# Four of eight low one-hot groups: subtraction on GpSimd and two activations on ScalarE in place of VectorE's comparison

## The reference, cut to what matters

```python
shared = _ffn(xf, shared_gate, shared_up, shared_down)
probs = softmax(xf @ gate_w.T)
topw, topi = top_k(probs, 2)
topw = topw / (topw.sum(-1, keepdims=True) + 1e-20)
comb = zeros((T, E)).at[arange(T)[:, None], topi].add(topw)
for e in range(E):
    routed += _ffn(xf, expert_gate[e], expert_up[e], expert_down[e]) * comb[:, e][:, None]
return shared + routed
# _ffn(x, g, u, d) = silu(x @ g.T) * (x @ u.T) @ d.T
```

## Time and profile before

| | us |
|---|---|
| median of three runs | 841.98 (841.88 to 842.23) |
| profiled execution | 840.84 |
| its span, first to last instruction | 839.1 |
| busy in the span: PE | 783.3 (93%) |
| DVE | 588.7 (70%) |
| ACT | 487.4 (58%) |
| POOL | 277.0 (33%) |
| mean granted clock of TensorE | 0.987 of full |

### The profile page before, as it was taken

How to read it: one execution, slowest core, us unless ns; L and a number is a source line. 1 busy time by engine, 2 the same in 40 slices (tenths; PEclk the granted TensorE clock), 3 DMA queues, 4 the chain that set the end, 5 groups by cost and what they waited for, 6 DMA issues and landing times.

```text
span 839.1 us, 21195 instructions
## 1 busy us (share of the span) xinstructions
PE 783.3 (93%) x6686; PEld 642.8 (77%) x6695; DVE 588.7 (70%) x1568; ACT 487.4 (58%) x1073; POOL 277.0 (33%) x301
## 2 busy tenths in 40 slices
PE   6989999999999997778999999999999999999990
PEld 3547777777777776666888888888888888888880
DVE  5758989898989898897888644555555555555552
ACT  3364848484857576533466655565656565656561
POOL 3011010101010101002565555555555555555542
PEclk9999999999999999999999999999999999999996
DMA  4114444444444343203264567856464646464633
GB/s 194 51 36 172 113 145 114 145 122 153 119 148 129 132 115 130 45 14 90 53 171 77 98 70 72 123 96 131 76 152 72 148 69 151 74 147 68 147 39 94
DMA packets 102708, 90.11 MB, mean 107 GB/s; under 512 B 63776, under 2 KB 94240, under 8 KB 101472
## 3 DMA queue, kind: packets, MB, share of 16 engines
q1 hardware_dynamic: 87664, 68.45, 28.7%
q0 software_dynamic: 14976, 20.78, 17.5%
HBM read 48.70 MB, written 27.39 MB: 91 GB/s over the span
## 4 chain that ended last, share of the span: by engine, by line
PE 73%; DVE 15%; issue 5%; ACT 5%; POOL 1%; DMA 1%; ACTq 0%; DVEq 0%; POOLq 0%
PE ps L948 41%; PE ps L963 19%; PE ps L1067 4%; PE ps L1099 3%; DVE wgu L1355 3%; DVE hf L1295 2%; PE ps L1061 2%; ACT wgu L805 2%; DVE wdn L1355 1%; DVE st L1537 1%; DVE att L1462 1%; PE ps L1028 1%; DVE hT L1305 1%; DVE st L1275 1%; PE ps L1070 1%
## 5 line engine op out<-in xcount | busy, mean ns | idle before, releaser
L948 PE MATMUL ps<-xhl,wgu 128*128 128x256 f16 x3102 | 383.6, 273 | 7.0 <-DVE hf L1295 5.2
L948 PEld LDWEIGHTS ps<-xhl,wgu 128*128 (+1 forms) x3102 | 301.8, 98 | 50.4 <-DVE hf L1295 6.8
L1295 DVE SCALAR_TENSOR_TENSOR hf<-ps,sc,silu 128x256 f32<-128x256 f32 x330 | 159.7, 484 | 172.4 <-ACT silu L755 146.2
L963 PE MATMUL ps<-wdn,hT 128*128 (+1 forms) x1870 | 253.3, 273 | 11.3 <-DVE hT L1305 8.5
L755 ACT ACTIVATE silu<-ps,sc 128x256 f32<-128x256 f32 x275 | 130.0, 473 | 226.2 <-PE ps L948 223.0
L963 PEld LDWEIGHTS ps<-wdn,hT 128*128 128x128 f16 x1870 | 180.9, 98 | 38.0 <-DVE hT L1305 7.6
L696 POOL DMA_INDIRECT acc_d<-ysb,gst x78 | 128.6, 1649 | 44.5 <-POOL gst L692 30.9
L641 POOL TENSOR_TENSOR rstd<-ve,mhalf 128x4 f32<-128x4 f32 (+1 forms) x32 | 30.7, 959 | 294.2 <-DVE ve L1280 272.5
L769 ACT CAST hT<-hf 128x256 f16<-128x256 f32 x275 | 109.7, 399 | 12.1 <-DVE hf L1295 10.1
L1305 DVE TENSOR_TENSOR hT<-hf,hT 128x256 f16<-128x256 f32 x275 | 114.8, 417 | 1.7
L685 POOL DMA_INDIRECT attw<-xn_d,gst x74 | 75.9, 1025 | 42.1 <-POOL gst L681 30.9
(11 more groups left out here) (242 smaller groups left out, 775.3 us busy)
## 6 DMA issues: line engine op xcount, KB each, us to landing
wgu<-in_gu SPq DMA_DIRECT2D x8, 1408.0 KB, 6.2
att<-in_x SPq DMA_DIRECT2D x16, 512.0 KB, 5.6
wdn<-in_dn SPq DMA_DIRECT2D x8, 768.0 KB, 8.2
x_d<-att SPq DMA_DIRECT2D x8, 512.0 KB, 2.9
xn_d<-wgu SPq DMA_DIRECT2D x8, 512.0 KB, 3.4
acc_d<-ysb SPq DMA_DIRECT2D x16, 256.0 KB, 3.3
att<-x_d SPq DMA_DIRECT2D x8, 512.0 KB, 4.8
att<-acc_d SPq DMA_DIRECT2D x7, 512.0 KB
```

Source lines behind the costliest of these rows:

```text
L948: ins = te.matmul(o, slot_gu(slot, hw, k, j), x(hx, k), start=(n == 0), stop=(n == len(TERMS) - 1))
L963: ins = te.matmul(y_bank(u, tt), h(hh), slot_dn(slot, c, hw), start=(c == 0 and n == 0 and tt == 0), stop=(c == FC - 1 and n == 1 and tt = ...
L1295: v.scalar_tensor_tensor(out=hf[lo:P, c % 2 * TW:(c % 2 + 1) * TW], in0=up, scalar=scale_of(slot, 1, lo, P), in1=silu[lo:P, c % 2 * TW:(c ...
```

## The change

For groups 3, 4, 5 and 6 the comparison on DVE is replaced. POOL subtracts the column numbers from the low parts (tensor_tensor, subtract) into oh_lo[g], as soon as lo16 of the first seven batches is there (lo_ready), one group behind the other with no wait between them. ACT then takes the absolute value in place, waits for it, and writes relu(1 - x) in place, which is 1 where the difference was 0 and 0 where it was another whole number. The four ACT pairs are steps act_lo in TAIL. DVE keeps groups 0, 1, 2 and 7. The list is written anew in its middle: the inverts 4 to 7 come ahead of D 5, and route_indices 0 ahead of G 8 rather than behind H 7.

```diff
+POOL_LO = (3, 4, 5, 6)
-        ("H", 2), ("D", 1), ("route_slots", 1), ("one_lo", 1), ("route_weights", 1), ("G", 4), ("H", 3), ("D", 2), ("route_positions", 1), ("one_hi", 0),
-        ("G", 5), ("H", 4), ("D", 3), ("one_lo", 2), ("one_lo", 3), ("invert", 0), ("invert", 1), ("G", 6), ("H", 5), ("D", 4), ("one_lo", 4), ("one_lo", 5),
-        ("G", 7), ("H", 6), ("D", 5), ("invert", 2), ("invert", 3), ("one_lo", 6), ("one_lo", 7), ("one_hi", 1), ("G", 8), ("H", 7),
-        ("invert", 4), ("invert", 5), ("invert", 6), ("invert", 7), ("route_indices", 0), ("D", 6), ("G", 9), ("H", 8), ("D", 7), ("route_counts",), ("G", 10),
+        ("H", 2), ("D", 1), ("act_lo", 3), ("route_slots", 1), ("one_lo", 1), ("route_weights", 1), ("G", 4), ("H", 3), ("D", 2), ("act_lo", 4), ("route_positions", 1), ("one_hi", 0),
+        ("G", 5), ("act_lo", 5), ("H", 4), ("D", 3), ("invert", 0), ("invert", 1), ("one_lo", 2), ("one_lo", 7), ("one_hi", 1), ("G", 6), ("act_lo", 6), ("H", 5), ("D", 4),
+        ("invert", 2), ("invert", 3), ("G", 7), ("H", 6), ("invert", 4), ("invert", 5), ("invert", 6), ("invert", 7), ("D", 5),
+        ("route_indices", 0), ("G", 8), ("H", 7), ("D", 6), ("G", 9), ("H", 8), ("D", 7), ("route_counts",), ("G", 10),
...
+            pool.wait_ge(rows2_made, B)
+            pool.wait_ge(rows2_hi, B)
+            pool.wait_ge(x2_stored, 16 * B)
+            pool.wait_ge(lo_ready, 1)
+            for n in POOL_LO:
+                g.tensor_tensor(oh_lo[n], *compared(n), ALU.subtract).then_inc(pool_lo_made, 1)
...
+                if step[0] == "act_lo":
+                    n = POOL_LO.index(step[1])
+                    act.wait_ge(pool_lo_made, n + 1)
+                    a.activation(oh_lo[step[1]], oh_lo[step[1]], ACT.Abs).then_inc(act_lo_made, 1)
+                    act.wait_ge(act_lo_made, 2 * n + 1)
+                    a.activation(oh_lo[step[1]], oh_lo[step[1]], ACT.Relu, bias=ones[:, 0:1], scale=-1.0).then_inc(act_lo_made, 1)
...
-                pe.wait_ge(onehot_lo_made, g + 1)
+                if g in POOL_LO:
+                    pe.wait_ge(act_lo_made, 2 * POOL_LO.index(g) + 2)
+                else:
+                    pe.wait_ge(onehot_lo_made, g + 1 - sum(p < g for p in POOL_LO))
...
-                    v.tensor_copy(both(lo16), both(lohi_i[:, :]))
+                    v.tensor_copy(both(lo16), both(lohi_i[:, :])).then_inc(lo_ready, 1)
```

More of the change, by code:

```diff
@@ L335, in build @@
         onehot_lo_made = sem("onehot_lo_made")
+        pool_lo_made = sem("pool_lo_made")
+        act_lo_made = sem("act_lo_made")
+        lo_ready = sem("lo_ready")
         comb_made = sem("comb_made")
@@ L597, in _, with compared @@
             sp.wait_ge(out_stored, 16 * (B + 1))
+        def compared(g):
+            shape = [P, 2, OHB, P]
+            l4 = lo16.rearrange("p (m j o) -> p m j o", m=2, o=1)[:, :, OHB * g:OHB * (g + 1), :].to_broadcast(shape)
+            i4 = iota16[:, :].rearrange("p (a b c) -> p a b c", a=1, b=1).to_broadcast(shape)
+            return l4, i4
         @block.gpsimd
@@ L1457, in one_lo @@
             def one_lo(g):
[L1459 to L1462, removed]
+                v.tensor_tensor(oh_lo[g], *compared(g), ALU.is_equal).then_inc(onehot_lo_made, 1)
             def route_indices(n):
```

## The result

The changed kernel takes 847.79 us (847.56 to 848.72, four runs) where the kernel before takes 842.11 (841.88 to 842.43): ratio 1.0069, 95% interval 1.0052 to 1.0087, so 5.7 us slower, clear of the 0.2% that can be told. In the three sets of runs made later the kernel before had medians of 842.34 to 843.06 us, against which the same time would be 4.7 to 5.5 us more, so the size is known to about a microsecond. The profiled execution has a span of 845.8 us, against 839.1.

The account below looks back on a forecast made before the run. DVE was taken as the bound from 350 to 373 us, with PE waiting for it. Relief -0, ACT 0 and shut-out 7.3 gave +7.3 us on the profiled 840.84, 848.1; 1.14 for the median made 849.3 us, range 841.0 to 852.5.

Parts of the forecast that it names:

- the case of no loss at all: Rival 1's case: DVE not held up by POOL's subtractions, 841.98 us with 841.4 at best; chance 0.26.
- What comes off DVE: Four comparisons, 4.9 us, leave DVE's stretch; 0 to 0.6 us reach PE, taken as 0.
- the walk: Undisturbed step-by-step timing from DVE's high half at 363.49 through H5 to D6 at 373.9 to 374.6; worth 0 to 0.6 us.
- most of it is spent in the new wait: Most of DVE's 4.9 us relief goes into its wait for PE's inversions, ahead of route_indices 0.
- The gathers: Could start at about 373.3 instead of 376.13, G0 of the first routed tile at 384.3, but L1149 waits for route_order.
- What is added to ACT: Eight activations of 128x1024, 8.5 us beside a little-busy ACT; cost 0, silu 4 free by 1.8 us.
- The shut-out: POOL's reads block DVE's two-SBUF-input instructions between 349.3 and about 360: 7.3 us, bounds 2.9 and 10.5; chance 0.52.
- Rival 1: DVE is not shut out beside POOL's subtractions and the walk holds: 841.98 us, 841.4 at best; chance 0.26.
- rival 2: DVE is held up in part, POOL letting go between its pieces: +3.7 us, so 845.6; chance 0.10.
- Rival 3: DVE not shut out, relief reaching further: the gathers' chain would give all of 2.8 us, 839.2; chance 0.09.
- rival 4: POOL needs over 3.8 us per subtraction, ACT waits, silu 4 is late; adds to the shut-out, over 852; chance 0.03.
- The evidence against an exclusion: At 33.70 a two-input DVE instruction, begun 0.02 us after POOL's power, took its usual 0.19 us.

Follow-up runs that it names:

- e2: The changed kernel without POOL's subtractions, groups 3 to 6 of the one-hots zero, so their tokens are left out; 843.18 us, ratio 1.0007 to the kernel before.
- e9: The kernel of e2 run once more, beside its control e11 and e10 on one chip; 841.87 us, ratio 0.9990.
- e8: e2 with inverts 4 to 7 and route_indices back behind G 8 and H 7; 842.78 us, ratio 1.0004.
- e10: The kernel of e8 run once more; 842.04 us, ratio 0.9987.
- e1: The kernel before with only POOL's four subtractions added, DVE keeping all eight comparisons and ACT getting nothing; 847.37 us, ratio 1.0064.
- e4: The kernel before with eight POOL memsets of 128x1024 at the place of e1's subtractions; 843.71 us, ratio 1.0012.
- e3: Control for e2: the kernel before, with DVE's comparisons of groups 3 to 6 giving zeros at the same price; 842.42 us, ratio 0.9997.
- e11: The kernel of e3 run once more, as control beside e9 and e10; 842.21 us, ratio 0.9994.

## Why the prediction was right

The direction and the mechanism held, the size was 7.3 us forecast and 5.7 us measured, and the range (841.0 to 852.5), which had to take in the case of no loss at all, held the time. By its steps:

- **What comes off DVE** (0): right as far as the timed runs can tell, not in its parts. From H4 on, the walk forecast H5 3.6 us behind H4, and it is 374.30 - 370.66 = 3.64. It forecast D6 10.4 to 11.1 us behind H4, and it is 381.65 - 370.66 = 10.99. In between, L1498 came at 8.23 us (8.1 to 8.7 forecast), and H7 1.80 us behind it in place of 1.4, for it waited 0.31 us for its silu. DVE waits 1.67 us for the inversions ahead of L1498, where 2 to 3 us were forecast. But the walk was for an undisturbed kernel, which is e2 and e9, and there D6 comes 26.39 and 26.31 us behind the lo16 cast; the walk's range is 24.9 to 25.6. It allowed 0.6 us for a low clock, and in both profiles PE was at 1.2 GHz from D3 over G6 to D4 (1.46, 2.72 and 1.44 to 1.49 us). Put back in the old place (e8, e10), route_indices brings nothing that the timed runs can tell, and 0.6 to 0.7 us of the stage at the same clock. So "most of it is spent in the new wait" named only one place. With that wait gone, DVE waits for PE's pieces instead: 3.37 us ahead of H7 in e8, and 1.36 ahead of H6 and 2.93 ahead of H7 in e10, where PE's clock was low.
- **The gathers**: as forecast, G0 of the first routed tile comes right behind the fillers, and L1178 then waits for route_order (1.26 us <-DVE upper L1665). Their place ahead of G 8 is worth nothing.
- **What is added to ACT** (0): right in the sum, wrong in the slack. The first activation takes 1.05 us, the second 1.15. Silu 4 starts at 370.06 and ends 0.15 us before DVE wants it, where I had 1.8 us. The shut-out delayed G3 and silu 3 with it, and at 1.2 GHz G3 took 2.76 us. ACT had no room for a longer instruction there.

Rival 1 (not shut out) fell with e1; rival 2 (half) fell with the four rows, each of which waits to the end of a subtraction. Rival 3 fell with e2 and e9, rival 4 with the 1.90 us.

The evidence against an exclusion, POOL's power at 33.68 beside a small DVE instruction, is no single case. In the same trace another power starts at 332.10, and DVE starts L1305, which reads hf and hT, 0.23 us later at its usual length:

```profile
332.10 1.01 POOL L641 TENSOR_TENSOR rstd<-ve,mhalf 128x4 f32<-128x4 f32 x1 [8.65 <-DVE ve L1280]
...
332.33 0.41 DVE L1305 TENSOR_TENSOR hT<-hf,hT 128x256 f16<-128x256 f32 x1
```

The prediction set these aside because a power of four columns reads little and then computes. The runs bear that out so far as copies and subtractions of 1024 columns hold DVE up to their end; what decides between the two kinds was not tested.

## What to carry to other kernels

POOL is no free engine for elementwise work beside a DVE that is the bound: each of its subtractions and copies of 1024 columns held up DVE's next instruction with two SBUF inputs, however small that was, until it was done (a power of four columns did not). Before moving work to POOL, count DVE's two-input instructions in the stretch where it will run, and price the move at POOL's own duration, less what DVE can do beside it without a second SBUF input (here 7.6 less 2.1 us). And where several engines take turns, four instructions less on one of them can be worth nothing that a timing shows: walk the next waits before counting a relief, once with PE at 2.4 GHz and once at 1.2.

## What was not expected of the hardware

A POOL memset, which reads nothing, held up a DVE cast with a single input from 0.19 to 1.01 us (e4), while two-input instructions beside it ran on as usual. So beside the reads there seems to be a second way of colliding, of a cast against writes; it was seen once.

The lock goes both ways within one stretch: one_lo 0 waited 1.18 us for POOL's first subtraction, and the second subtraction waited 0.97 us for one_lo 0.

A drop of TensorE to 1.2 GHz falls on other pieces in other profiles of one and the same kernel: G6 took 1.47 us in e3 and 2.72 in e11, 1.47 in e8 and 2.72 in e10. In the kernel with four comparisons off DVE (e8, e10) that moves the stage by 1.01 us without any edit, more than most of the effects that were looked for here; in the control (e3, e11) by 0.09 us. The 1.7 us by which such a drop was said to move things, in the expectation of e9, is the difference between e2 and e8, and 0.6 to 0.7 us of it are the order of the list.
